# One core, two fused transformer layers: new step places and zero products, maximum rows of the first head pair copied inside SBUF, maxima issued one unit ahead

## The reference, cut to what matters

```python
x = x + ga * _L0_attn_ref(h, Wq, Wk, Wvdown, Wvup)     # one head, causal
x = x + gb * _L0_ffn_ref(h, Wg, bg, We, be)            # argmax picks an expert
q, k, v = (16 heads of width 8)                        # layer 1
weight = softmax(einsum('bimd,bjmd->bmij', q*s, k*s))  # 1024 x 1024 per head
x = x + ga * (einsum('bmij,bjmd->bimd', weight, v) @ Wout.T + bout)
x = x + gb * _L1_ffn_ref(h, W1, b1, W2, b2)
```

## Time and profile before

| | us |
|---|---|
| median of 3 runs | 1739.2 (1736.26 to 1743.79) |
| the profiled execution | 1754.4 |
| its span, first to last instruction | 1753.0 |
| TensorE busy | 1621.5 |
| VectorE busy | 1495.7 |
| ScalarE busy | 1370.7 |
| mean granted TensorE clock, share of full | 0.962 |

### The profile page before, as it was taken

How to read it: one execution, slowest core, us unless ns; L and a number is a source line. 1 busy time by engine, 2 the same in 40 slices (tenths; PEclk the granted TensorE clock), 3 DMA queues, 4 the chain that set the end, 5 groups by cost and what they waited for, 6 DMA issues and landing times.

```text
span 1753.0 us, 55013 instructions
## 1 busy us (share of the span) xinstructions
PE 1621.5 (92%) x23302; PEld 670.6 (38%) x23313; DVE 1495.7 (85%) x2256; ACT 1370.7 (78%) x1934; POOL 678.4 (39%) x1085
## 2 busy tenths in 40 slices
PE   5769899999999999999999999999999999988998
PEld 2543343334334443334334343334334342223224
DVE  4649988999889998999889998999889998899853
ACT  4442678987899878987899878987899877777774
POOL 2421335445534365444534365345544362002010
PEclk9998999999999999999999999999999998899888
DMA  2120101112210311112210311112110311011100
GB/s 72 51 65 25 61 31 51 35 47 70 79 35 24 90 55 51 36 45 68 72 46 20 94 55 51 36 42 71 54 53 17 95 45 62 22 33 47 41 17 23
DMA packets 83281, 87.10 MB, mean 50 GB/s; under 512 B 9452, under 2 KB 67484, under 8 KB 83036
## 3 DMA queue, kind: packets, MB, share of 16 engines
q1 hardware_dynamic: 82492, 83.07, 15.8%
q10 hardware_dynamic: 544, 0.52, 0.1%
HBM read 61.02 MB, written 21.99 MB: 47 GB/s over the span
## 4 chain that ended last, share of the span: by engine, by line
PE 59%; DVE 18%; ACT 13%; issue 6%; POOL 3%; DMA 1%; SPq 0%; ACTq 0%; POOLq 0%; DVEq 0%
PE pv_psum L798 20%; PE side_psum L526 15%; PE buffer L783 11%; DVE row_max L1335 11%; ACT p L1011 8%; PE buffer L773 6%; PE side_psum L616 2%; PE buffer L526 2%; PE side_psum L583 2%; ACT o_sb L1020 1%; DVE idx L1207 1%; DVE s L1181 1%; POOL xn_f L1371 1%; DVE st_f L1074 1%; DVE top L1201 1%
## 5 line engine op out<-in xcount | busy, mean ns | idle before, releaser
L1335 DVE TENSOR_REDUCE row_max<-buffer 128x2 f32<-128x1024 f32 x1024 | 1223.0, 1218 | 133.3 <-PE buffer L773 120.2
L1011 ACT ACTIVATE p<-buffer 128x1024 f32<-128x1024 f32 x1024 | 1044.0, 1026 | 206.1 <-PE buffer L783 193.3
L798 PE MATMUL pv_psum<-p,v 128*9 128x256 f32 x8192 | 606.9, 396 | 6.1 <-ACT o_sb L1020 2.9
L773 PE MATMUL buffer<-k_ops,q_ops 24*128 24x512 f16 x2048 | 410.7, 398 | 35.5 <-ACT p L1011 23.4
L783 PE MATMUL buffer<-q_ops,k_ops 26*128 26x512 f16 x2048 | 409.3, 397 | 20.6 <-DVE row_max L1335 18.2
L798 PEld LDWEIGHTS pv_psum<-p,v 128*9 128x9 f32 x8192 | 153.5, 90 | 251.9 <-issue 172.3
L783 PEld LDWEIGHTS buffer<-q_ops,k_ops 26*128 26x128 f16 x2048 | 96.5, 91 | 398.7 <-issue 245.5
L773 PEld LDWEIGHTS buffer<-k_ops,q_ops 24*128 24x128 f16 x2048 | 96.9, 91 | 156.3 <-ACT p L1011 119.3
L1481 POOL TENSOR_SCALAR nm_parts<-nm 128x16 f16<-128x16 f32 x64 | 19.1, 298 | 342.2 <-DVE nm L1258 342.2
L1466 POOL TENSOR_TENSOR hm<-masks,hT_f 128x1024 f32<-128x1024 bf16 x56 | 120.3, 2149 | 55.5 <-PE side_psum L526 52.3
L526 PE MATMUL side_psum<-we,hm 128*32 128x128 f32 x3648 | 122.8, 276 | 2.4 <-issue 2.4
(11 more groups left out here) (309 smaller groups left out, 1622.1 us busy)
## 6 DMA issues: line engine op xcount, KB each, us to landing
masks<-masks_rows SPq DMA_DIRECT2D x16, 1024.0 KB, 5.6
q_ops<-products SPq DMA_DIRECT2D x256, 48.0 KB
k_ops<-products SPq DMA_DIRECT2D x256, 48.0 KB
attention<-o_sb SPq DMA_DIRECT2D x248, 18.0 KB
x<-in_L_attn_inputs SPq DMA_DIRECT2D x8, 512.0 KB, 4.5
products<-q_parts SPq DMA_DIRECT2D x16, 256.0 KB, 2.3
w_sb<-in_L_ffn_W SPq DMA_DIRECT2D x16, 256.0 KB, 2.9
out<-x SPq DMA_DIRECT2D x16, 256.0 KB, 2.3
```

Of the source, the lines that this page charges most:

```text
L773: m = e.matmul(buffer[:, hh, :], q_ops[rows, slot, of, i * P:(i + 1) * P], k_ops[rows, slot, of, halves(half)[1]], start=True, stop=True)
L798: m = e.matmul(pv_psum[q:q + VW, half * QUARTER:(half + 1) * QUARTER], v1[b % 2][:, kb, 2 * hp + hh, :], p_sb[n % KEPT][:, hh, part * QUAR ...
L1011: e.activation(p_sb[n % KEPT][:, :, :], unit("exp", n)[0][:, :, :], ACT.Exp, scale=over_scale[n // (2 * PERIOD)]).then_inc(S["exp_done"], 1)
L1335: e.tensor_reduce(mx[pair % 2][:, :, i, half], unit("max", n)[0][:, :, :], axis=AX.X, op=ALU.max).then_inc(S["max_done"], 1)
```

## The change

Five things change.

1. `PLACES` gives 99 of the 191 stages another step, most by one to three; `COUNTED`, `SWITCH` and `LIGHT` change too, so some value units move to a neighbouring step.
2. Zero products: `keep_busy` now takes 256 columns instead of 512. Ahead of stages of the lists there are 264 instead of 44 (`ZEROS_AHEAD`); in the steps below zero 128 of 256 columns instead of 64 of 512; in 70 of the steps 834 to 1019 there are 151 new ones of four tiled products each, into the side bank (`zeros_beside`).
3. The rows of the first pair for the maxima are copied from `q_parts` and `k_parts` straight to `q_ops` and `k_ops`, in 24 small transfers issued by SP and ACT, and `max_scores` of that pair waits for these alone. `load_operands(0)` reads four transfers instead of eight.
4. In `ALONE`, the second half of k goes ahead of that of q.
5. In the steps below zero the maxima on TensorE are one unit ahead of the side products.

```diff
-SWITCH, LIGHT = 1.2, 5.4
+SWITCH, LIGHT = 1.4, 5.7
...
-BUSY_AHEAD = {("channels", 0, 1, 1): 12, ("channels", 0, 2, 1): 10, "steps": 4, ("channels_b", B - 1, 0): 16, ("ffn", B - 1, 0): 2, ("ffn", B - 1, 1): 2}
+ZEROS_AHEAD = {
+    "steps": 12, "channels_b 7 0": 36, "ffn 7 0": 13, "channels 0 1 1": 33, "channels 0 2 1": 23, "onehotT 0 1": 4, "scores 0 7 0": 4, "moe_a 0 2": 2,
...
+ZEROS_BESIDE = {
+    -32: 2, -30: 3, -27: 2, -26: 3, -24: 4, -22: 6, -21: 3, -20: 2, -19: 1, -18: 2, -17: 10, -16: 5, -15: 1, -14: 2, -13: 6, -12: 6, -11: 5, -10: 6,
+    -9: 3, -8: 5, -7: 7, -6: 8, -5: 5, -4: 10, -3: 10, -2: 4, -1: 7, 834: 3, 837: 3, 839: 2, 841: 3, 844: 1, 846: 3, 850: 1, 851: 2, 852: 2, 854: 1,
...
-scores 1 2 0, channels 0 2 1, transpose_p 1 1 0, qk1 0 0 1, apply 0 2 1, softmax 1 2, parts 0 0 1, qk1 0 1 1, scores 1 3 0, v1 0 1, exp0 1 2,
-parts 0 1 1, transpose_p 1 2 0, times_v 1 1, sums0 1 0, exp0 1 3, scores 1 4 0, scores 1 4 1, transpose_p 1 3 0, transpose_p 1 3 1, softmax 1 3,
+scores 1 2 0, channels 0 2 1, transpose_p 1 1 0, qk1 0 1 1, apply 0 2 1, softmax 1 2, parts 0 1 1, qk1 0 0 1, scores 1 3 0, v1 0 1, exp0 1 2,
+parts 0 0 1, transpose_p 1 2 0, times_v 1 1, sums0 1 0, exp0 1 3, scores 1 4 0, scores 1 4 1, transpose_p 1 3 0, transpose_p 1 3 1, softmax 1 3,
...
+def maxima_at(h):
+
+    if h >= 0:
+        return range(h + 2 * LEAD, min(h + 2 * LEAD + 1, PAIRS * UNITS))
+    due = [min(h + 2 * LEAD + ahead, 2 * LEAD) for ahead in (EARLIER, EARLIER + 1)]
+    return range(0 if h == -2 * LEAD else due[0], due[1])
...
+    def straight_operands(queue, w, half, heads):
+
+        cols = halves(half)[1]
+        done = S["first_half" if half == 0 else ("first_queries", "first_keys")[w]]
+        for hh in heads:
+            for r, part in enumerate((Q_PART, K_PART)[w]):
+                row = MAX_ROWS + ROW_TILE * hh + DH * r
+                queue.dma_start((q_ops, k_ops)[w][row:row + DH, 0, 0, cols], qk1_parts[w][DH * hh:DH * (hh + 1), part, cols]).then_inc(done, 16)
...
-                for first_row in (MAX_ROWS, EXP_ROWS):
+                for first_row in (MAX_ROWS, EXP_ROWS) if g else (EXP_ROWS,):
...
-                e.matmul(pv_psum[:, :], ident_bf[:, :], zero[:, :].broadcast_to([P, BANK]), start=True, stop=True)
+                e.matmul(pv_psum[:, 0:QUARTER], ident_bf[:, :], zero[:, :].broadcast_to([P, QUARTER]), start=True, stop=True)
...
+        def zeros_beside(last_side, count):
+
+            pe.wait_ge(S["side_" + last_side.by], last_side.emptied)
+            for n in range(count):
+                for q in range(0, P, COLUMN_TILE):
+                    e.matmul(side_psum[q:q + COLUMN_TILE, 0:QUARTER], ident_bf[:, q:q + COLUMN_TILE], zero[:, :].broadcast_to([P, QUARTER]), start=True, stop=True)
...
         def parts(b, w, half):
-            if (b, w) == (0, 1):
+            if b:
+                return
+            if half:
+                act.wait_ge(S[f"split{w}_1"], 1)
+                act.wait_ge(S["operands_set"], 2)
+                straight_operands(e, w, 1, (1,))
+            if w:
                 act.wait_ge(S[f"split1_{half}"], 1)
                 store_parts(e, b, w, half, slice(0, 1))
```

More of the change, by code:

```diff
@@ L26 @@
 KEPT, LAG, LAG_MOST = 6, 2, 5
+EARLIER = 1
 EPS = 1e-5
@@ L115 @@
[L115 to L118, removed]
@@ new lines @@
+maxima 4, 52 nm_split 4, 53 nm 4, 67 maxima 5, 68 nm_split 5, 70 nm 5, 85 maxima 6, 83 nm_split 6, 90 nm 6, 95 maxima 7, 94 nm_split 7, 100 nm 7, 80
+load_w12 0, 98 wout 0, 95 w2T 0, 97 wff_a 0, 98 wff 0, 116 x_bias 0, 134 sums_load 0, 141 sums 0, 137 sums_out 0, 146 sums_in 0, 143 numerators 0 0,
+145 numerators 0 1, 151 wout_mm 0 0, 154 wout_mm 0 1, 161 stats_b 0 0 0, 161 stats_b 0 0 1, 163 stats_b 0 1 0, 161 apply_b 0 0, 164 stats_b 0 1 1, 165
+apply_b 0 1, 168 x_wff 0, 167 channels_b 0 0, 169 ffn 0 0, 170 channels_b 0 1, 172 ffn 0 1, -207 stats 0 0 0 0, -199 stats 0 0 0 1, -195 stats 0 0 1
@@ new lines @@
+0, -193 stats 0 0 1 1, -195 apply 0 0 0, -193 apply 0 0 1, -192 channels 0 0 0, -191 g0 0 0, -190 channels 0 0 1, -188 g0 0 1, -189 v0 0, -189 later
+0, -193 gates 0, -187 scores 0 0 0, -185 softmax 0 0, -184 exp0 0 0, -185 scores 0 1 0, -183 transpose_p 0 0 0, -182 softmax 0 1, -181 exp0 0 1, -180
+scores 0 2 0, -179 transpose_p 0 1 0, -178 softmax 0 2, -182 times_v 0 0, -177 exp0 0 2, -176 scores 0 3 0, -175 transpose_p 0 2 0, -174 softmax 0 3,
+-174 times_v 0 1, -173 exp0 0 3, -166 sums0 0 0, -172 scores 0 4 0, -171 scores 0 4 1, -170 transpose_p 0 3 0, -168 transpose_p 0 3 1, -168 softmax 0
@@ L812, in tensor_program @@
                 early[name, *at]()
-            if (name, *at) in BUSY_AHEAD:
-                keep_busy(BUSY_AHEAD[name, *at])
+            zeros_ahead(name, *at)
             if name in stages:
                 stages[name](*at)
-        keep_busy(BUSY_AHEAD["steps"])
+        zeros_ahead("steps")
         for bank, u in before_steps.items():
@@ L823, in tensor_program @@
                 exp_scores(h)
-            if h + 2 * LEAD < PAIRS * UNITS:
-                max_scores(h + 2 * LEAD)
+            for n in maxima_at(h):
+                max_scores(n)
             for n in values_at.get(h, ()):
@@ L830, in tensor_program @@
                     stages[name](*at)
-            if h < 0:
-                keep_busy(1 if h < -LEAD else 3)
+            sides = [side[stage] for stage in plan.get(h, ()) if stage in side]
+            side_now = sides[-1] if sides else side_now
+            open_side = any(name.endswith("_a") for name, *at in plan.get(h, ()))
+            if ZEROS_BESIDE.get(h) and not open_side:
+                if h < 0:
+                    keep_busy(ZEROS_BESIDE[h])
+                else:
+                    zeros_beside(side_now, ZEROS_BESIDE[h])
         for name, *at in last:
-            if (name, *at) in BUSY_AHEAD:
-                keep_busy(BUSY_AHEAD[name, *at])
+            zeros_ahead(name, *at)
             if name in stages:
@@ L1604, in parts @@
             sp.wait_ge(S[f"split{w}_{half}"], b + 1)
+            if b == 0:
+                sp.wait_ge(S["operands_set"], 2)
+                straight_operands(e, w, half, (0,) if half else (0, 1))
             if b >= 2:
```

56 lines of the change are left out of this document (35 added, 21 removed), and 21 rows, old and new, of tables (COUNTED, ZEROS_AHEAD, ZEROS_BESIDE).

## The result

| | before | after |
|---|---|---|
| median (21 executions each) | 1736.7 us (1732.3 to 1743.8) | 1745.6 us (1740.2 to 1750.3) |
| the profiled execution, its span | 1754.4, 1753.0 | 1746.25, 1744.9 |
| its mean granted clock | 0.962 | 0.987 |
| mean granted clock of the timed executions | 0.961 to 0.981 | 0.983 to 0.990 |

What follows compares the result with a forecast made beforehand. TensorE work was taken to bind the steady periods and, at low clock, the last sequence. Terms -11 (zeros beside steps), -2 (end), -2 (start), 0 (places) sum to -15 us, 1724 from the 1739.2 median; range 1706 to 1741.

Steps and rivals of the forecast that it cites:

- The stretch at the low clock: Last sequence, 1475 to 1697 us: 66.6 us at the low level; a clock held full gives back 16.1 us.
- rival A: Zeros don't hold the clock in full, or plain runs lack most low stretches: 1735 us, no change; chance 0.24.
- The zeros' visible time: Steps 834 to 990: 16 us of TensorE time for zeros, partly covered by its idle time; 5 us visible, bounds 0 and 16.
- Does a zero hold the clock?: Last sequence: tiled zeros resemble the side products of periods at clock 0.98 to 0.99, so they should hold the clock.
- the rule that I weighed: Clock falls come from long idle gaps between products, so zeros where no such gap exists change nothing; kept as a rival.
- The prediction's reading of the fall: At 1476 us the clock was said to fall after three microseconds in which TensorE was busy 2.03.
- The straight copies: Start of the maxima: landing -2.7, longer list +2.8, zeros +0.5, about +0.5 us in all; bounds -2.7 and +4.
- One unit ahead and the start: Steps below zero: less VectorE idle time, perhaps a full clock, -2.5 us (0 to -4); start in all -2 us.
- The zeros in the lists: Hand-written lists: 264 zeros fill waits of TensorE, 0 us (-2 to +3).
- Places: New places and counts in the periods: 0 us, bounds -8 and +8 over 6.5 periods.
- Rival C: New places and counts shorten each period by 1.5 of 8 idle us: -10 more, 1714 us or below; chance 0.18.
- The end: Last steps and last list: clock gain against zeros on the path, net -2 us, bounds -5 and +3.

Runs made afterwards that it cites:

- e5: The kernel before with only the new PLACES, COUNTED, SWITCH and LIGHT; median 1750.0 us, ratio to before 1.0054.
- e2: The changed kernel without the 151 zeros in steps 834 to 1019; median 1747.9 us, ratio to before 1.0031.
- f1: The changed kernel with straight copies and k-before-q order undone and no zeros from step 834 on; 1745.0 us, ratio to before 1.0044.
- g4: The changed kernel with straight copies and k-before-q order undone and 35 zeros beside the last steps; 1736.6 us, ratio to before 0.9978.
- h1: The same kernel as g4, timed again on another chip; median 1740.0 us, ratio to before 0.9991.
- h2: As h1, but with the old places, counts and constants; median 1737.6 us, ratio to before 0.9973.
- e4: The kernel before, unchanged, timed and profiled again; median 1738.9 us, ratio to before 0.9997.
- e1: The changed kernel with straight copies and k-before-q order undone, first pair's maximum rows again through DRAM; 1738.5 us, ratio to before 0.9989.
- f3: The same kernel as e1, with 151 zeros, timed again as base for other zero amounts; 1741.1 us, ratio to before 1.0003.
- e3: The kernel before with only the 151 zeros in steps 834 to 1019 added; median 1744.4 us, ratio to before 1.0019.
- g3: The changed kernel with straight copies and k-before-q order undone, 70 zeros beside the last steps, lists' zeros as before; 1742.1 us, ratio to before 1.0011.
- second group: Four follow-up kernels on the start and the places, timed beside the kernel before on one chip; ratios to before 1.0010 to 1.0062.

## Why the prediction was wrong

Two steps failed, and both count: less was gained from the clock than forecast, and more was paid for it.

**The stretch at the low clock was taken for the kernel's own.** This step failed in the sentence "carried over whole the sum gives 1724". For the profiled execution the term was sized about right: after step 832 the low time fell from 78.5 to 10.2 us, which at 0.29 is worth 20 us (16 at the prediction's 0.24). But most of that low time belonged to the one execution. The kernel before, profiled again, had 13.7 us, and the six other executions with no zeros or 35 beside the steps (e5, e2, f1, g4, h1, h2) 17.1 to 34.1. The forecast counts about 21 us for the clock (16.1 here, 2.5 at the end, 2.5 at the start). In timed executions it was worth about 11: after's mean clock is 0.987, and on the line above before's 1736.7 us lie between 0.976 and 0.977. The warning stood in the text, the 15 us between profile and median, and was kept as the reason of rival A instead of being subtracted. Rival A's first half ("plain runs lack most of the low stretches") is what happened.

**The zeros' visible time** was 5 us of 16 ("Bounds: 0 and 16 us; I take 5"), and this is the other step that failed. The price of one was right, 0.11 us against 0.12, though by luck in part: the 0.13 of the earlier trace rows is for four products of 128 columns, and a zero has four of 256. All 151 are 16.7 us, and 9 to 12 of them were visible, not a third. What was wrong is the cover: TensorE's idle time stayed where it was (17.8 and 18.0 us without and with zeros in 1475 to 1697 us) instead of being used up.

**Does a zero hold the clock?** Yes, as held against the rule that I weighed: with 0, 70, 151 and 302 zeros the lowest clock of the timed executions is 0.962, 0.980, 0.981 and 0.984. By the line, the clock that 70 zeros hold is worth 13 us, for 4.7 paid; 151 add 1 us to that and 5.3 to the price. So the idea was sound and the amount too large. TensorE's busy share in 1475 to 1697 us is about the same with none (204.24, e4) and 151 (202.45), and its longest idle stretch there was 0.8 us in before and in e4, where the clock fell. The page "TensorE: Matmul & The Clock Gate" of the Trainium skill (section "HAM oscillation — how this bites in real kernels") puts the fall down to long idle gaps, and by that the zeros would change nothing here; these runs disagree. What it is in the zeros that holds the clock stays open. The prediction's reading of the fall was off as well: in the earlier trace rows the clock is still 1.00 up to 1476 us, and the window behind it is

```profile
1476.00:1479.00 3.00, 3.00 (x29) 0.82 (x27) 3.00 (x3) 2.24 (x5) 0.00 (x0) 0.84 0.14 30
```

so the clock fell inside this window, in which TensorE was busy throughout, and the 2.03 of 3 us did not stand right before the fall.

**The straight copies** were +0.5 us of start (bounds -2.7 and +4) and measured +4.2. Two sizes were wrong. A copy on ScalarE's queue took 0.95 us (2.85 for three) while SP took 0.66 for each of its three, where I had 0.42 to 0.67 from queues that issued alone; the q evacuation moved by 4.15 - 1.17 = 3.0 us, past my 2.4. And what is removed is less than the 2.7 us of waiting: 1.3 is left of it in e1, once the list carries its further zeros. The ratios of after, e1 and f3 (1.0041, 0.9989, 1.0003) would make it 8 us; at equal clock it is 4.5, as in the profile.

**One unit ahead and the start.** -2.5 was forecast, and no gain is shown. The stretch to the first exponential shrank by 1.9, but e3 shows 46.4 us for the old program when no low time falls there. The same holds for the clock in 131 to 150 us: it rose from 0.64 to 0.91, and e3 has 1.00 there with nothing changed. The zeros below step 0 (128 of half size for 64) were not tried by themselves. The zeros in the lists were 0 and delay the last `hT_f` by 0 to 1.5.

**Places** were 0. Rival C's price is partly there (the period is shorter by half a us), but not its mechanism: it took TensorE's 8 idle us of a period to shrink, and they grew to 9; what fell is the time at the low level. The gain is repaid below step 0 and, by 2 us, in the last sequence, so that at equal clock the places cost 0 to 3.5 us. After's further 2 us of its 5.5 over steps 0 to 832 fall in the first 16 (24.7 us instead of 26.6). That is the places', not the clock's: of the profiled executions with 3.4 low us in these 16 steps, before, e4 and h2 (old places) take 26.5 to 26.6 us, and after, e5, g3, g4 and h1 (new ones) 24.5 to 25.1.

**The end** was -2 and measured +0.5 (19.6 against 19.1).

Together, in timed executions: about 11 us gained from the clock where 21 were forecast, and about 19 paid at equal clock where 6 were. Of the 19, the zeros beside the steps are 10, the copies 4 to 5, and the new places with the lists' zeros the rest (f1: 5.6). That is +8 us, against +7 by the ratio and +9 by the medians.

## What to carry to other kernels

One profiled execution whose mean clock differs from the timed ones tells of itself. Before a gain is read from a low stretch, compare its time with the median of plain executions, and subtract what the clock explains; a second profile of the same kernel costs little. Time each execution beside its mean clock: a line through the unchanged kernel's executions separates what a change costs from what the clock gives, and here it explained differences that medians of twelve left open. Idle time of an engine is not free room: see whether it shrinks when work is put in. Filler work beside a bound engine was paid for with over half of its time here: try it at none, half, once and twice, and stop at the smallest that steadies the clock. Transfers that an engine's own queue issues can hold up that engine's next instruction (4.15 us here instead of 1.17), so give them to an idle queue.

## What the runs showed of the hardware that I had not expected

- The same kernel ran at mean granted clocks from 0.961 to 0.985 on one chip, and its time went with it, 1727.8 to 1751.7 us over the 26 executions of before that the ratios of the second group count.
- In e4, 1730.2 us at 0.981 to 1751.3 at 0.961 is 21 us for 2 x 0.020 x 1740 = 70 us at the low level, 0.30 us each, as in the two profiles of before (0.29) and above the 0.24 that the steps give.
- Copies inside SBUF of 8 rows cost ScalarE's queue 0.95 us each where SP's queue issued its own at 0.66 at the same time, and 0.65 to 0.82 each a little later. Six in a row on SP alone took 3.98 us.
- A zero of four 32-column tiles and 256 columns costs TensorE 0.11 us among other products, alone or in groups of up to six.
- Twelve executions of kernels with the same zeros in the list reach a fixed point of it, the last `hT_f`, between 111.1 and 117.3 us.
